# Moving the adds of two node stages, and one scaling, from VectorE to GpSimd in a four-layer graph network

## What is computed

```python
h = jnp.maximum(_layernorm(x, axis=-1), 0.0)
x = x + layer(h, edges)          # a message per edge, added up at the edge's target node
```

```python
h = jax.nn.relu(_layernorm(x, ln_g, ln_b))
agg = jax.ops.segment_sum(msg, dst, num_segments=N)
return agg + h @ Wr + bias
```

## Time and profile before

| | |
|---|---|
| median of 3 runs | 4295.58 us |
| the profiled execution | 4291.38 us, its span 4289.6 us |
| node stage of layer 2 | about 2355 to 2497 us of the span |
| node stage of layer 3 | about 3189 to 3286 us of the span |

### The profile page before, as it was taken

The page is one execution under the profiler, slowest core; times in us unless marked ns, Lnnn a source line. Parts: engine busy times, 40 slices in busy tenths (PEclk is TensorE's granted clock), DMA queues, the critical chain, the costliest instruction groups (busy, mean ns, idle before and its releaser), DMA issues.

```text
span 4289.6 us, 28738 instructions
## 1 busy us (share of the span) xinstructions
PE 2171.9 (51%) x7442; PEld 1517.8 (35%) x7442; DVE 2886.2 (67%) x4329; ACT 1192.7 (28%) x2949; POOL 2739.8 (64%) x2799
## 2 busy tenths in 40 slices
PE   1200035545300005888887046667651666767998
PEld 1100024444300003555555035555540444444444
DVE  8892036666570005888888867777767888877887
ACT  1000023333420003333343234444422433430110
POOL 3777777777777777655653056666622777764776
PEclk7555567777655557999999568888875888889999
DMA  6011023333630001222223322222343333351110
GB/s 178 9 31 46 8 59 109 110 102 109 101 101 5 5 5 45 83 83 79 87 83 86 98 69 91 90 89 83 90 95 111 107 98 107 107 95 43 35 35 26
DMA packets 200521, 321.19 MB, mean 75 GB/s; under 512 B 83898, under 2 KB 166698, under 8 KB 199971
## 3 DMA queue, kind: packets, MB, share of 16 engines
q1 hardware_dynamic: 112848, 265.61, 17.3%
q0 software_dynamic: 82368, 21.64, 7.7%
q10 hardware_dynamic: 5140, 32.09, 2.0%
HBM read 66.90 MB, written 252.21 MB: 74 GB/s over the span
## 4 chain that ended last, share of the span: by engine, by line
POOL 38%; DVE 23%; issue 19%; PE 17%; DMA 1%; SPq 1%; ACT 0%; DVEq 0%; POOLq 0%
POOL rows L464 20%; DVE work L1130 9%; POOL edges_by_dst L448 9%; POOL edges_by_src L448 9%; PE psX L653 7%; PE psX L560 6%; DVE psX L1160 3%; DVE natD L1155 2%; DVE psX L1176 2%; PE psX L576 2%; DVE h L1020 1%; PE psK L551 1%; DVE psX L1017 1%; PE psK L630 1%; DVE x L1214 0%
## 5 line engine op out<-in xcount | busy, mean ns | idle before, releaser
L464 POOL DMA_INDIRECT rows<-table,rec x1792 | 1693.0, 945 | 1087.1 <-issue 519.2
L551 PE MATMUL psK<-work 128*128 128x224 f32 x3584 | 896.1, 413 | 576.5 <-DVE work L1112 298.1
L551 PEld LDWEIGHTS psK<-work 128*128 128x128 f32 x3584 | 822.1, 234 | 719.7 <-issue 666.4
L1130 DVE SCALAR_TENSOR_TENSOR work<-work,keep,psK 128x224 f32<-128x224 f32 x1792 | 800.9, 447 | 87.3 <-PE psK L551 15.9
L560 PE MATMUL psX<-natD 128*128 128x512 f32 (+1 forms) x1120 | 608.4, 678 | 340.4 <-DVE natD L1168 150.0
L760 ACT ACTIVATE work<-iota,rec 128x128 f32<-128x128 f32 x1792 | 545.9, 391 | 576.2 <-PE psK L551 358.9
L448 POOL DMA_INDIRECT edges_by_dst<-natD,pos x391 | 374.7, 958 | 184.2 <-issue 127.0
L1112 DVE TENSOR_TENSOR work<-at_hi,psX 128x1792 f32<-128x1792 f32 x224 | 452.2, 2019 | 6.1 <-ACT psX L802 0.3
L448 POOL DMA_INDIRECT edges_by_src<-natS,pos x391 | 374.4, 958 | 128.1 <-issue 128.1
L587 PE MATMUL psX<-ident,rows 128*128 128x128 f32 x168 | 51.6, 307 | 767.3 <-DMA rows<-table,rec 767.3
L560 PEld LDWEIGHTS psX<-natD 128*128 128x128 f32 x1120 | 231.4, 229 | 556.5 <-DVE natD L1168 176.3
(11 more groups left out here) (147 smaller groups left out, 2342.6 us busy)
## 6 DMA issues: line engine op xcount, KB each, us to landing
scan<-work SPq DMA_DIRECT2D x224, 896.0 KB
rows<-table,rec POOLq DMA_INDIRECT x1792
table<-h ACTq DMA_DIRECT2D x28, 896.0 KB, 3.6
work<-scan SPq DMA_DIRECT2D x168, 112.0 KB, 2.0
rec<-edges_by_dst SPq DMA_DIRECT2D x112, 84.0 KB, 1.9
natD<-scan SPq DMA_DIRECT2D x56, 112.0 KB, 2.0
edges_by_dst<-natD,pos POOLq DMA_INDIRECT x391
edges_by_src<-natS,pos POOLq DMA_INDIRECT x391
```

The source lines that it names most:

```text
L464: pool.indirect_dma_start(out=rows[k][:, u * D:(u + 1) * D], out_offset=None, in_=table.ap(), in_offset=bass.IndirectOffsetOnAxis(ap=rec[k ...
L551: nc.tensor.matmul(psK[:, o:o + BW], at_lo[par][:, t * P:(t + 1) * P], spread[par][:, t * BW:(t + 1) * BW], start=True, stop=True)\
L1130: V.scalar_tensor_tensor(acc[par][:, t * BW:(t + 1) * BW], was, keep[s][:, bass.ds(q * G + t, 1)], psK[:, o:o + BW], ALU.mult, ALU.add).th ...
```

## The change

The adds of the edges' sums in layers 2 and 3, and in layer 2 the last multiplication by the reciprocal root, are taken from VectorE's program and put into GpSimd's, ahead of its wait for the stores. `sdev2` and `mean2` change places in memory: `mean2` is now in PSUM (GpSimd must read `sdev2`, which stays in SBUF). A semaphore `inverse` tells GpSimd that the reciprocal is there.

```diff
+                if l >= 2:
+                    n = nd[l]
+                    for c in range(NCH + 2):
+                        if c < NCH:
+
+                            xs = at_chunk(x, c)
+                            pool.wait_ge(n[f"load{c % 2}"], 16 * PER * (c // 2 + 1))
+                            nc.gpsimd.tensor_tensor(xs, xs, tin[c % 2], ALU.add).then_inc(n["took"], 1)
+                        if l == 2 and c >= 2:
+                            hs = v3(at_chunk(h, c - 2))
+                            pool.wait_ge(n["inverse"], c - 1)
+                            nc.gpsimd.tensor_tensor(hs, hs, sdev2[:, :, None].to_broadcast([P, CH, D]), ALU.mult)\
+                                .then_inc(n["norm"], 1)
+
                 pool.wait_ge(nd[l]["store"], 16 * NCH)
...
+        mean2 = psX[:, 2 * CH:3 * CH]
...
                         if l == 3:
-                            load_wait(n, c)
-                            V.tensor_tensor(xs, xs, tin[c % 2], ALU.add).then_inc(n["took"], 1)
                             dve.wait_ge(n["took"], c + 1)
...
                         xs = at_chunk(x, c)
-                        load_wait(n, c)
-                        V.tensor_tensor(xs, xs, tin[c % 2], ALU.add).then_inc(n["took"], 1)
                         dve.wait_ge(n["took"], c + 1)
                         mean_of(xs, means[c % 2])
...
                     if c >= 2:
-                        hs = at_chunk(h, c - 2)
                         dve.wait_ge(n["sdev"], c - 1)
-                        own.did(V.reciprocal(sdev2, sdev2))
-                        own.settle()
-                        V.tensor_tensor(v3(hs), v3(hs), bc(sdev2), ALU.mult).then_inc(n["norm"], 1)
+                        V.reciprocal(sdev2, sdev2).then_inc(n["inverse"], 1)
```

More of the change, by code:

```diff
@@ L192, in build_gnn @@
         small2 = natS[:, 4096:4096 + 4 * CH]
+        sdev2 = small2[:, 3 * CH:4 * CH]
         wide = [natS[:, i * 1024:(i + 1) * 1024] for i in range(4)]
@@ L249, in build_gnn @@
         nnames = ("load0", "load1", "scaled", "mixed", "relu", "took", "center", "square", "varsum", "sdev", "norm",
[L250 to L253, removed]
+                  "floor", "center2", "square2", "varsum2", "inverse", "store")
+        lacks = [("load0", "load1", "scaled", "mixed", "relu", "took", "floor", "center2", "square2", "varsum2",
+                  "inverse"), ("floor", "center2", "square2", "varsum2", "inverse"), ("scaled", "mixed", "varsum"),
+                 ("scaled", "mixed", "relu", "floor", "center2", "square2", "varsum2", "inverse")]
         nd = [{n: sem(f"n{l}_{n}") for n in nnames if n not in lacks[l]} for l in range(4)]
@@ L678, in _ @@
             var = small[:, CH:2 * CH]
-            total2, sdev2 = small2[:, 2 * CH:3 * CH], small2[:, 3 * CH:4 * CH]
+            total2 = small2[:, 2 * CH:3 * CH]
             def square(n, c, which=""):
@@ L1010, in _ @@
             var = small[:, CH:2 * CH]
-            mean2, floor2, total2, sdev2 = [small2[:, i * CH:(i + 1) * CH] for i in range(4)]
+            floor2, total2 = [small2[:, i * CH:(i + 1) * CH] for i in (1, 2)]
             def load_wait(n, c):
```

## The result

| | before | after |
|---|---|---|
| median of 10 runs each | 4296.01 us | 4308.14 us |
| lowest to highest | 4289.44 to 4304.22 | 4302.31 to 4317.86 |
| ratio, 95% interval | | 1.003 (1.0018 to 1.0042) |
| profiled execution | 4291.38 | 4314.2 |

The change makes the kernel 0.3% slower, 12 us: inside the range given, on the side forecast, 3 us under the forecast. The single parts of the sum came out less well than the whole.

What follows compares the result with a forecast made beforehand. A node stage was taken to cost its chain up to the last store of `h`, mostly VectorE's work. Layer 2 +18.5 and layer 3 -2.8 gave +15.7 us on 4295.58, so 4311 us, range 4303 to 4319.

Steps and rivals of the forecast that it cites:

- The mechanism: Layer 2, iterations 2 to 6: GpSimd's multiplication and next add stay between VectorE's iterations, costing 16.4 us more.
- The rival of work beside VectorE: Layer 2: the next add is done during VectorE's iteration, saving 16.1 us at the crossings; 4279 us, chance 0.03.
- The multiplication's price: Layer 2's multiplication on GpSimd was priced like its plain add, 3.98 us, between bounds of 1.98 and 4.42.
- a multiplication clearly off 4 us: A sign named ahead that would show the prediction wrong: GpSimd's multiplications in the changed profile not near 3.98 us.
- a crossing: Layer 2, from the reciprocal's end to the next mean, into iterations 3 to 6: 8.12 us instead of 4.02.
- Nothing lost, nothing won: Layer 2's start: chunk 1's mean starts 2.0 us later, chunk 2's missing add makes up for it.
- The end: Layer 2, iterations 7 and 8: multiplication, store and last root follow one another, the last multiplication ending 2.1 us later.
- Layer 3: SP's load issues set the pace, so chunk 6's mean comes 2.8 us earlier, not the 14.4 that leave VectorE.
- The rule weighed: VectorE instructions with two SBUF inputs contend with GpSimd's SBUF reads, the later one blocked; nothing was added for it.
- the rival of a faster SP: Layer 3: SP issues at its undisturbed pace, gaining 7.2 us instead of 2.8; 4307 us, chance within the forecast's.
- The cheap rival: Layer 2: the repeated operand costs GpSimd no reads, multiplication 1.98 us; 4301 us, halfway (3 us) 4306, chance 0.1.
- the dear multiplication: Layer 2: short runs make GpSimd's multiplication take 6 us, the five bring +10; 4321 us, chance 0.07.

Runs made afterwards that it cites:

- e4: The full change, but GpSimd issues the add of chunk c+1 ahead of the multiplication of chunk c-2; ratio to the kernel before 0.9991.
- e8: The full change with GpSimd's add ahead of its multiplication, floor2 in PSUM, the last two multiplications on VectorE; ratio to before 0.9964, repeated 0.9976 (4286.27 us).
- e9: As e8, and VectorE centres chunk c before summing the second variance of chunk c-2; 4280.05 us, ratio to the kernel before 0.9962.
- e5: The full change with GpSimd's multiplication as whole-tensor multiplication (even chunks) or repeated-operand addition (odd); layer 2's stage 146.09 us, no ratio.
- e3: The full change with layer 2's last multiplication back on VectorE, so only both layers' adds on GpSimd; ratio to the kernel before 0.9992.

## Why the prediction was right, and where its steps were not

**The mechanism held.** GpSimd's pair stands between VectorE's iterations, four times, and only there; e4 shows that it is the order, since with the add ahead VectorE's 7.27 us of idling vanish. The rival of work beside VectorE could not come true in this program, as said, but is what e4, e8 and e9 make of it.

**The multiplication's price was mis-sized.** I took the plain add's 3.98 us between bounds of 1.98 and 4.42. It is 3.24, and by the signs named ahead a multiplication clearly off 4 us was one of being wrong. I had named the repeated operand as what could make it cheaper and dismissed it with the nearest form; the middle of the bounds would have served better. The argument that an operand read again and again would save nothing does not hold either: e5 shows 0.72 us saved. With 3.24 a crossing costs 3.25 us more (7.27 instead of 4.02) and not 4.1; 13.0 in all, not 16.4.

**"Nothing lost, nothing won" at the start was wrong by 2.2 us.** I followed VectorE's own instructions, whose mean of chunk 2 was to start as before, and did not ask what else stood behind the missing add. It had covered ScalarE's relu and square. VectorE now arrives early and waits 1.42 us; the floor's hold adds 0.67. From the first landing to the first reciprocal it is 37.46 us, against 35.27. The error has the opposite sign of the two others. Crossings and end were set 4.9 us too dear (3.4 and 1.5), this gives 2.2 back, and layer 2's stage comes to +15.8 instead of +18.5. So the forecast of 4311 owes some of its closeness to luck.

**The end** was to cost 2.1 us and costs 0.65 (from the last but one reciprocal to the last multiplication's end 9.07 us, before 8.42). The path was right, through the store and the root on ScalarE; the cheaper multiplication, which stands in it twice, makes 1.5 us.

**Layer 3** came out as read: chunk 6's mean 61.68 us behind the first landing, before 64.52, so -2.84 where -2.8 was said. SP's issues took 65.64 us for 56, whatever VectorE's speed; at the undisturbed pace that the rival of a faster SP named it would have been 61.

**The rule weighed** was dismissed too soon. I looked only for instructions with two SBUF inputs, and took the one that remained for harmless; it is, in the change (0.13 us longer, while the root waits for the store anyway). The floor, with one source and no operand in PSUM, was not looked at and cost 0.67; it is of the other kind that the Trainium skill names, told above. In e3 and e4 such holds are worth 5.9 and some 9 us (four holds of L1093, 1.49 and three times 2.45, and the first floor 0.55).

The cheap rival's halfway price of 3 us would have given 4306, and the measured 4308.14 lies between that and the forecast; the dear multiplication did not happen.

What stays open: why a repeated operand saves 0.72 us on GpSimd; what separates the VectorE instructions that are held from the reciprocal, which is not; and what sets the scatter of layer 2's edge stage, 706 to 715 us with one code.

## What to carry to other kernels

Moving work to an idle engine helps where the waiting engine does not need it next: look at the order in the helper's program, since an operation that is ready may stand behind one that is not. Then check what the removed operation had been hiding on a third engine, and whether an instruction of one engine is held by the other's; here one operand in PSUM removed that. Measured by stages, from a landing to the first gather, repeated kernels agree to 0.1 us, so effects of 0.3 us can be read that the total of a run can't show.

## What the runs showed of the hardware

A GpSimd instruction with two whole 1792-element inputs took 3.96 us and one with an operand repeated over 16 elements 3.24, for addition and multiplication alike. Three VectorE instructions were held until a running GpSimd instruction had ended: the floor (one source, SBUF to SBUF, 0.22 us alone, up to 2.85 held), the sum of L1089 (two SBUF inputs, 0.27 alone, 2.72 held) and the multiplication (two SBUF inputs, 2.02 alone, 3.09 held). With one operand in PSUM the two small ones took 0.28 and 0.27 us beside GpSimd. The hold goes by who is first: VectorE's 1.96 us add, 0.16 us ahead, drew GpSimd's multiplication from 3.24 to 4.89 us. Reductions, centres with the mean in PSUM, and the one reciprocal that met an add (0.84 us) were not held.
